# Layer 1's attention: GpSimd issues each half group's eight gathers only when the half group ahead has landed

## The chip, the core and the metric

The kernel runs on one core of a Trainium2 chip. A core has five engines that run their own instruction streams side by side and meet only at semaphores: TensorE (PE, matrix products and transposes, with weight loads shown as PEld), VectorE (DVE), ScalarE (ACT), GpSimd (POOL) and SyncE (SP, which here only issues DMAs). Sixteen DMA engines move data between HBM and the on-chip memory. The metric is the device time of one execution in microseconds (us). Before the change the median of three runs is 1322.91 us (1320.9 to 1323.34).

## The reference

Two layers work on 128 graphs of 64 nodes with 256 features, which is 8192 tokens. Each layer is a graph attention and a mixture of experts, both added to their input:

```python
# --- layer 0 ---
x = x + _L0_gnn_ref(_layernorm(x), adj, L0_gnn_W, L0_gnn_a)
x = x + _L0_ffn_ref(_layernorm(x), router_w, w1, b1, w2, b2)   # 8 experts, best 2, hidden 256, gelu
# --- layer 1 ---
x = x + _L1_gnn_ref(_layernorm(x), adj, L1_gnn_W, L1_gnn_a)
x = x + _L1_ffn_ref(_layernorm(x), Wg, bg, bias, W1, b1, W2, b2)  # 8 experts, best 2, hidden 512, relu

def _L1_gnn_ref(x, adj, W, a):
    Wh = jnp.einsum('bnf,fo->bno', x, W)
    a1, a2 = (a[:F_out, 0], a[F_out:, 0])
    e = (Wh @ a1)[:, :, None] + (Wh @ a2)[:, None, :]
    e = jnp.where(e > 0, e, ALPHA * e)
    attention = softmax(jnp.where(adj > 0, e, NEG_BIG), axis=-1)
    return elu(jnp.einsum('bij,bjo->bio', attention, Wh))
```

The change sits where layer 0 ends and layer 1's attention begins: x after layer 0 is x plus, for each token, its two best experts' outputs, each multiplied by its gate.

## The kernel before, in words

All tokens stay on the chip in the array X, in 64 tiles of 128 tokens (two graphs a tile). A group is 8 tiles, a half group is 4; there are 8 groups and 16 half groups.

Layer 0's experts write their outputs into a table in HBM, `expert_outputs` (`yslots` in the code), sorted by expert. Layer 1's attention begins with the way back. For each tile t and each of the two choices k, `gather_outputs` lets GpSimd issue one indirect DMA (L597) that fetches 128 rows of 256 floats, 128 KiB, into a ring of 16 tiles in the array WREG (`ring0`). That is 8 gathers for a half group and 128 in all. Four semaphores `y_gathered` are used in turn, one for a half group, and each gather adds 16 to its own, so that 8 gathers add 128. From the 17th tile on, every second tile waits at L594 for a transposition on TensorE (`xT_mm`), since a place in the ring is free only when its old tile has been added and transposed. GpSimd issues groups in order. Behind group 1 it writes two small tables (`one_hot_rows`, L605), and behind groups 3 to 7 it computes the low part of one expert weight (`low_part`, L611).

VectorE takes a half group with `add_outputs` (L1275 to L1287): it waits until the half group's semaphore shows all eight gathers, multiplies and adds the four tiles' first choices, then their second choices, and gives the mean to ScalarE. ScalarE sums the squares (`squares`, L1037), VectorE makes the inverse root (`first_rstd`, L1316 to L1325), and TensorE transposes (`turn_x`, L769) and projects (`project`, L782). ScalarE scales the projected rows (`scale_rows`, L1021).

VectorE's program has a fixed order. It takes half groups 0, 1, 2 and 3 (with the inverse roots of group 0 between them) before its first softmax, that of group 0 (`soft`, L1336). Within group g it then takes the two half groups of group g + 2: the first behind the division of the probabilities (`normalise_probs`, L1350), the second behind the first `add_relu` (L1360). The text below numbers half groups from 0 to 15, so half group 2 is the first half of group 1, and group 2 is half groups 4 and 5.

Of the kernel before, what the change touches and what calls it, by code (L numbers as in the profile page):

```python
# [61 lines left out]
def at(n):  # L62

    return n + AHEAD


def build(nc, x_in, adj, W_gnn, a_gnn, router, gate_b, gate_bias, w1, b1, w2, b2, out):

    ctx = ExitStack()
    with ctx:  # L70
# [3 lines left out]
        def sem(name):  # L74
            return ctx.enter_context(nc.semaphore(name))
# [143 lines left out]
        y_gathered = [sem(f"y_gathered_{k}") for k in range(4)]  # L219
# [288 lines left out]
        def _(pool):  # L508
# [56 lines left out]
            for L in range(2):  # L565
# [24 lines left out]
                def gather_outputs(g):  # L590

                    for t in range(g * GT, (g + 1) * GT):
                        if t >= 2 * GT and t % 2 == 0:
                            pool.wait_ge(xT_mm[1], at((t - 12) // 2 + 1))  # L594
                        for k in range(TOPK):
                            o = (TOPK * (t % (2 * GT)) + k) * D
                            nc.gpsimd.indirect_dma_start(  # L597
                                out=ring0[:, o:o + D], out_offset=None, in_=yslots,
                                in_offset=bass.IndirectOffsetOnAxis(ap=pos_i[k][:, t:t + 1].bitcast(U32), axis=0)
                            ).then_inc(y_gathered[t // 4 % 4], 16)  # L600
# [12 lines left out]
                if L == 0:  # L613
                    inverse_root(0)
                    no_edges(0)
                    inverse_root(1)
                    diagonal(0)
                    no_edges(1)
                    later_constants()
                    for g in range(1, GROUPS):  # L620
                        diagonal(g)
                        if g + 1 < GROUPS:
                            inverse_root(g + 1)
                        if g + 1 < GROUPS:
                            no_edges(g + 1)
                        cut_weights(g - 1, 0)
                        cut_weights(g - 1, 1)
                    cut_weights(GROUPS - 1, 0)
                    cut_weights(GROUPS - 1, 1)
                    pool.wait_ge(setup_dve, 2)  # L630
                    one_hot_rows()
                else:
                    for u in range(SU):
                        pool.wait_ge(stored[u], 16 + 16 * (SLOTS[0] // SU))
                    for g in range(GROUPS):
                        gather_outputs(g)
                        if g == 1:
                            one_hot_rows()
                        if g >= 3:
                            low_part((g - 3) // 2, (g - 3) % 2)  # L640
                    for g in range(GROUPS - 3, GROUPS):
                        low_part(g // 2, g % 2)
# [1129 lines left out]
```

## Time and profile before

| | |
|---|---|
| Median of three runs | 1322.91 us |
| Lowest and highest | 1320.9, 1323.34 us |
| Span of the profiled execution | 1413.2 us |
| Mean granted TensorE clock | 0.870 |
| Busy in the span: PE, DVE, ACT, POOL | 77%, 68%, 39%, 49% |
| Gathers of L597 | 128, 991 ns each on average |

The span runs from the first to the last instruction of the one execution that was recorded; for that execution the profile gives no other time. It is 90.3 us longer than the median of the runs without a profile. A timeline row of the profile gives the start from the span's begin, the busy time, the engine, the line, the operation with output and input, how many instructions the row merges, and in brackets the idle time ahead of it and what ended it. Busy time of a gather on GpSimd is the time in which GpSimd writes its descriptors, not the transfer.

### The profile page before, as it was taken

Reading aid. Unit: us, or ns where it says so; the run is one execution under the profiler, and the core shown is the slowest. Engines: PE = TensorE matmul, PEld = TensorE weight load, DVE = VectorE, ACT = ScalarE, POOL = GpSimd, SP = SyncE. Lnnn points to the kernel's source line nnn. Section 1 sums busy time; section 2 is a strip of 40 time slices with the busy share of each in tenths; the row PEclk is TensorE's granted clock in tenths of the full one; section 3 lists DMA queues with packets and bytes.
Section 4 is the critical chain, followed back from the end, with each engine's and each line's share of the span. In section 5 each row is a group of like instructions: output and inputs, shape, how many; then the busy total and the mean of one; then the engine's idle time right before and its main releaser. Section 6 shows DMA issues by size and latency. Waiting matters only on the chain.

```text
span 1413.2 us, 31628 instructions
## 1 busy us (share of the span) xinstructions
PE 1090.2 (77%) x9392; PEld 894.5 (63%) x9393; DVE 963.9 (68%) x1851; ACT 550.3 (39%) x1229; POOL 696.6 (49%) x752
## 2 busy tenths in 40 slices
PE   6999482479999962556776486489999997799995
PEld 4777372468888852345564372377879886587774
DVE  4889688847777742568897888656666654466664
ACT  3666486422222211556776575022222222122221
POOL 3577681155555527546670380142533125776652
PEclk9999755589999995888889659599999998899998
DMA  9211151045555543234452553555767433443430
GB/s 283 55 46 39 60 179 60 13 120 158 160 157 158 163 131 102 71 83 139 117 158 59 162 181 104 47 168 163 209 178 177 138 110 113 128 129 119 122 111 12
DMA packets 126095, 172.53 MB, mean 122 GB/s; under 512 B 35109, under 2 KB 94000, under 8 KB 125744
## 3 DMA queue, kind: packets, MB, share of 16 engines
q0 software_dynamic: 28288, 83.03, 21.4%
q1 hardware_dynamic: 89504, 88.22, 19.9%
q10 hardware_dynamic: 8208, 0.07, 0.9%
q8 instruction: 53, 0.87, 0.3%
q14 instruction: 42, 0.34, 0.1%
HBM read 100.87 MB, written 71.44 MB: 122 GB/s over the span
## 4 chain that ended last, share of the span: by engine, by line
PE 52%; issue 19%; DVE 10%; POOL 5%; ACT 5%; another core or an unknown queue 4%; DMA 2%; SPq 1%; DVEq 1%; POOLq 0%; ACTq 0%
PE bank L964 20%; PE bank L978 18%; PE bank L782 5%; PE bank L947 4%; POOL arena L649 2%; ACT b_bc L1037 1%; PE bank L810 1%; DVE X L1279 1%; DVE arena L1623 1%; DVE stats L1269 1%; PE bank L900 1%; PE bank L800 1%; DMA stage_w<-in_L_ffn_W 1%; DVE arena L1624 1%
## 5 line engine op out<-in xcount | busy, mean ns | idle before, releaser
L1187 ACT ACTIVATE arena<-bank,b1T 128x256 f32<-128x256 f32 (+1 forms) x464 | 176.0, 457 | 565.2 <-PE bank L964 360.7
L964 PE MATMUL bank<-arena,WREG 128*128 128x256 f16 (+1 forms) x2784 | 323.8, 268 | 20.5 <-issue 17.9
L978 PE MATMUL bank<-WREG,arena 128*128 x2544 | 309.4, 275 | 35.8 <-issue 32.0
L978 PEld LDWEIGHTS bank<-WREG,arena 128*128 128x128 f16 x2544 | 247.1, 99 | 80.5 <-issue 48.8
L964 PEld LDWEIGHTS bank<-arena,WREG 128*128 x2784 | 253.0, 99 | 61.0 <-issue 31.6
L1693 DVE CAST arena<-arena 128x1024 f16<-128x1024 f32 (+1 forms) x140 | 83.9, 599 | 193.2 <-ACT arena L1187 154.8
L668 POOL DMA_INDIRECT arena<-split_tokens,gather_row x136 | 130.6, 960 | 148.7 <-PE bank L947 59.5
L782 PE MATMUL bank<-wg_sb,arena 128*128 128x258 f32 x512 | 142.9, 426 | 45.4 <-ACT arena L1010 29.0
L597 POOL DMA_INDIRECT WREG<-expert_outputs,pos_both x128 | 126.9, 991 | 99.4 <-PE bank L769 38.8
L679 POOL DMA_INDIRECT X<-token_rows,gather_row x72 | 73.5, 1021 | 176.0 <-DMA first_rows<-X 83.4
L782 PEld LDWEIGHTS bank<-wg_sb,arena 128*128 128x128 f32 x512 | 103.7, 212 | 71.8 <-ACT arena L1010 33.9
L1695 DVE TENSOR_TENSOR arena<-arena 128x1024 f16<-128x1024 f32 (+1 forms) x140 | 135.3, 966 | 4.8
L1705 DVE SCALAR_TENSOR_TENSOR arena<-bank,b_bc 128x512 f32<-128x512 f32 (+1 forms) x152 | 97.0, 645 | 50.6 <-PE bank L978 29.6
L679 POOL DMA_INDIRECT X<-first_rows,gather_row x72 | 75.8, 1052 | 87.6 <-DMA first_rows<-X 48.1
L1687 DVE COPY arena<-bank 128x1024 f16<-128x1024 f16 x140 | 95.4, 682 | 27.6 <-PE bank L947 11.8
L696 POOL DMA_INDIRECT out<-X,scatter_row x72 | 81.7, 1135 | 53.8 <-DVE X L1718 34.9
L1021 ACT ACTIVATE arena<-bank,minus_one,cols 128x258 f32<-128x258 f32 x128 | 71.0, 565 | 73.8 <-remote 28.4
L649 POOL TENSOR_TENSOR arena<-arena 128x512 f16<-128x512 f32 x64 | 75.6, 1192 | 45.1 <-DVE arena L1456 45.1
L861 PE MATMUL bank<-ident,arena 128*128 128x128 f16 x512 | 62.6, 298 | 38.4 <-POOL arena L649 37.6
L810 PE MATMUL bank<-arena 128*128 128x256 f32 x256 | 70.3, 411 | 17.6 <-ACT arena L1051 13.2
L1360 DVE SCALAR_TENSOR_TENSOR X<-bank,X 128x512 f32<-128x512 f32 x64 | 43.8, 685 | 51.9 <-ACT arena L1059 48.2
L1279 DVE SCALAR_TENSOR_TENSOR X<-WREG,cols,X 128x256 f32<-128x256 f32 x128 | 66.1, 574 | 17.4 <-DMA WREG<-expert_outputs,pos_both 15.6
(204 smaller groups left out, 1528.7 us busy)
## 6 DMA issues: line engine op xcount, KB each, us to landing
first_rows<-X SPq DMA_DIRECT2D x72, 257.0 KB, 4.6
expert_outputs<-arena SPq DMA_DIRECT2D x68, 256.0 KB
X<-in_x SPq DMA_DIRECT2D x16, 512.0 KB, 6.0
split_tokens<-arena SPq DMA_DIRECT2D x16, 512.0 KB, 2.9
stage_w<-in_L_ffn_W SPq DMA_DIRECT2D x16, 512.0 KB
token_rows<-X SPq DMA_DIRECT2D x8, 1024.0 KB
token_rows<-arena SPq DMA_DIRECT2D x16, 512.0 KB, 3.7
stage_w<-in_L_ffn_w SPq DMA_DIRECT2D x16, 256.0 KB, 2.7
```

The source lines that it names most:

```text
L597: nc.gpsimd.indirect_dma_start(out=ring0[:, o:o + D], out_offset=None, in_=yslots, in_offset=bass.IndirectOffsetOnAxis(ap=pos_i[k][:, t:t ...
L649: nc.gpsimd.tensor_tensor(y16_4[:, 2 * q:2 * q + 2, D:2 * D], y32_4[:, 2 * (q % 4):2 * (q % 4) + 2, :], y16_4[:, 2 * q:2 * q + 2, 0:D], AL ...
L668: nc.gpsimd.indirect_dma_start(out=gat[:, u * 512:(u + 1) * 512], out_offset=None, in_=table, in_offset=bass.IndirectOffsetOnAxis(ap=gathe ...
L679: nc.gpsimd.indirect_dma_start(out=token_row(ST * j + a, 0, ROW), out_offset=None, in_=first_rows if f else token_rows, in_offset=bass.Ind ...
L782: last = mm(Wh_bank(t), xT[:, b:b + P], wg(L, c, 0, WA), start=c == 0, stop=c == KC - 1)
L810: last = mm(bank[6 + q % 2][:, a * D:(a + 1) * D], probsT[:, j * P:(j + 1) * P], Wh[g % 2][:, j * WA:j * WA + D], start=True, stop=True)
L964: last = mm(hb, w1_at(L, ea, wh, kc, fc), tT[:, tb:tb + width], start=n == 0, stop=n == 3 * KC - 1)
L978: last = mm(ob[a], hsrc[:, h0:h0 + P], w2_at(L, e[a % len(e)], wh, fc), start=fc == 0 and n == 0, stop=fc == FC - 1 and n == 2)
L1187: ins = A(hid[:, h0:h0 + width], bank[2 + 2 * (u % 2) + fc // 2][:, b0:b0 + width], ACT.Gelu if L == 0 else ACT.Relu, bias=cut(b1T, ea * F ...
L1687: V.tensor_copy(tT[:, (u % 2) * 4 * SLOT:(u % 2 + 1) * 4 * SLOT], bank[u % 2][:].bitcast(F16)).then_inc(T_ev[L], 1)
L1695: tt(hid_lo[:, hb:hb + FC * SLOT], hid[:, hb:hb + FC * SLOT], hid_hi[:, hb:hb + FC * SLOT], ALU.subtract).then_inc(h_split[L], 1)
L1705: ins = stt(o_sb[:, o0:o0 + width].rearrange("p (a d) -> p a d", d=D), bank[6 + u % 2][:, a * width:(a + 1) * width].rearrange("p (a d) -> ...
```

## The change

Two lines are added to `gather_outputs`; nothing else changes. At each half group's first tile but the very first (15 times), GpSimd waits until the semaphore of the half group ahead shows all eight of its gathers.

```diff
@@ -590,6 +590,8 @@
                 def gather_outputs(g):
 
                     for t in range(g * GT, (g + 1) * GT):
+                        if t >= 4 and t % 4 == 0:
+                            pool.wait_ge(y_gathered[(t // 4 - 1) % 4], 128 * ((t // 4 - 1) // 4 + 1))
                         if t >= 2 * GT and t % 2 == 0:
                             pool.wait_ge(xT_mm[1], at((t - 12) // 2 + 1))
                         for k in range(TOPK):
```

No instruction moves on any engine. What changes is what GpSimd's gathers wait for. Before the change, GpSimd's program has the following rows from the start of layer 1 to the gathers of the 20th tile (`stored` are the semaphores of the stores to `expert_outputs`, `xT_mm_1` that of the transpositions, `x31` merges 31 equal rows):

```order
L597 DMA WREG<-expert_outputs,pos_both 128x256 [waits stored_2,stored_3,stored_1,stored_0]
L597 DMA WREG<-expert_outputs,pos_both 128x256 x31
L605 IOTA arena 128x256
L605 IOTA arena 128x288
L597 DMA WREG<-expert_outputs,pos_both 128x256 [waits xT_mm_1]
L597 DMA WREG<-expert_outputs,pos_both 128x256 x3
L597 DMA WREG<-expert_outputs,pos_both 128x256 [waits xT_mm_1]
L597 DMA WREG<-expert_outputs,pos_both 128x256 x3
```

After the change, the same stretch reads as follows; lines below the two new ones carry a number higher by 2, so the gather is L599 (`y_gathered_0` to `y_gathered_3` are the half groups' semaphores):

```order
L599 DMA WREG<-expert_outputs,pos_both 128x256 [waits stored_2,stored_3,stored_1,stored_0]
L599 DMA WREG<-expert_outputs,pos_both 128x256 x7
L599 DMA WREG<-expert_outputs,pos_both 128x256 [waits y_gathered_0]
L599 DMA WREG<-expert_outputs,pos_both 128x256 x7
L599 DMA WREG<-expert_outputs,pos_both 128x256 [waits y_gathered_1]
L599 DMA WREG<-expert_outputs,pos_both 128x256 x7
L599 DMA WREG<-expert_outputs,pos_both 128x256 [waits y_gathered_2]
L599 DMA WREG<-expert_outputs,pos_both 128x256 x7
L607 IOTA arena 128x256
L607 IOTA arena 128x288
L599 DMA WREG<-expert_outputs,pos_both 128x256 [waits xT_mm_1,y_gathered_3]
L599 DMA WREG<-expert_outputs,pos_both 128x256 x3
```

The unbroken row of 32 gathers is cut into four pieces of 8, and the gathers behind the small tables have two things to wait for. Further on, around the low part of a weight (L611 before, L613 after), GpSimd's rows after the change are:

```order
L599 DMA WREG<-expert_outputs,pos_both 128x256 [waits xT_mm_1,y_gathered_2]
L599 DMA WREG<-expert_outputs,pos_both 128x256 x3
L599 DMA WREG<-expert_outputs,pos_both 128x256 [waits xT_mm_1]
L599 DMA WREG<-expert_outputs,pos_both 128x256 x3
L613 TENSOR_TENSOR WREG<-stage_w,WREG 128x1024 [waits high_ready_1]
L599 DMA WREG<-expert_outputs,pos_both 128x256 [waits xT_mm_1,y_gathered_3]
L599 DMA WREG<-expert_outputs,pos_both 128x256 x3
```

There, every half group's first gather had a wait already and has a second one now; the low part stands between the two halves' boundary as before.

## Rows read from the trace of the kernel before

**Rows 1.** The page: length, and shares of the chain that ended last.

```profile
span 1413.2 us, 31628 instructions
...
PE 52%; issue 19%; DVE 10%; POOL 5%; ACT 5%; another core or an unknown queue 4%; DMA 2%; SPq 1%; DVEq 1%; POOLq 0%; ACTq 0%
```

**Rows 2.** Timeline of GpSimd, start of layer 1: the first 64 gathers.

```profile
522.89 0.94 POOL L597 DMA_INDIRECT WREG<-expert_outputs,pos_both  x1 [23.17 <-DMA expert_outputs<-arena]
...
531.64 0.95 POOL L597 DMA_INDIRECT WREG<-expert_outputs,pos_both  x1 [0.31 <-issue]
532.89 0.95 POOL L597 DMA_INDIRECT WREG<-expert_outputs,pos_both  x1 [0.30 <-issue]
...
561.91 0.94 POOL L597 DMA_INDIRECT WREG<-expert_outputs,pos_both  x1 [0.30 <-issue]
562.86 3.18 POOL L605 IOTA arena<- 128x256 bf16 x2
568.04 0.96 POOL L597 DMA_INDIRECT WREG<-expert_outputs,pos_both  x1 [2.00 <-remote]
...
576.94 1.06 POOL L597 DMA_INDIRECT WREG<-expert_outputs,pos_both  x1 [0.30 <-issue]
584.90 1.15 POOL L597 DMA_INDIRECT WREG<-expert_outputs,pos_both  x1 [6.90 <-PE bank L769]
```

**Rows 3.** Timeline of VectorE in the same stretch.

```profile
534.53 2.23 DVE L1279 SCALAR_TENSOR_TENSOR X<-WREG,cols,X 128x256 f32<-128x256 f32 x5 [13.57 <-DMA WREG<-expert_outputs,pos_both]
...
575.90 2.19 DVE L1279 SCALAR_TENSOR_TENSOR X<-WREG,cols,X 128x256 f32<-128x256 f32 x5
...
579.36 0.17 DVE L1287 TENSOR_SCALAR cols<-cols 128x4 f32<-128x4 f32 x1
583.81 0.69 DVE L1336 SCALAR_TENSOR_TENSOR arena<-no_edge,bank 128x512 f32<-128x512 uint8 x1 [4.29 <-PE bank L790]
```

**Rows 4.** The chain that ended last, in time order; last row: steady part.

```profile
543.83 9.87 another core or an unknown queue
...
554.29 9.90 another core or an unknown queue
...
564.78 2.94 another core or an unknown queue
...
568.21 2.06 ACT b_bc L1037 x8
...
593.60 14.37 another core or an unknown queue
...
726.58 0.22 another core or an unknown queue
```

**Rows 5.** Timeline of TensorE: the projections of group 0's first four tiles.

```profile
540.93 5.40 PE L782 MATMUL bank<-wg_sb,arena 128*128 128x258 f32 x16 [1.73 <-issue]
```

**Rows 6.** Timeline of ScalarE: the scaling of the second and third of these tiles.

```profile
553.72 0.56 ACT L1021 ACTIVATE arena<-bank,minus_one,cols 128x258 f32<-128x258 f32 x1 [9.89 <-remote]
564.21 0.57 ACT L1021 ACTIVATE arena<-bank,minus_one,cols 128x258 f32<-128x258 f32 x1 [9.92 <-remote]
```

**Rows 7.** Timeline of GpSimd in the steady part, groups 6 and 7.

```profile
699.44 0.95 POOL L597 DMA_INDIRECT WREG<-expert_outputs,pos_both  x1 [0.30 <-issue]
702.45 0.94 POOL L597 DMA_INDIRECT WREG<-expert_outputs,pos_both  x1 [2.06 <-PE bank L769]
...
711.96 0.95 POOL L597 DMA_INDIRECT WREG<-expert_outputs,pos_both  x1 [0.30 <-issue]
712.92 2.13 POOL L611 TENSOR_TENSOR WREG<-stage_w,WREG 128x1024 f16<-128x1024 f32 x1
715.22 0.97 POOL L597 DMA_INDIRECT WREG<-expert_outputs,pos_both  x1 [0.16 <-issue]
```

**Rows 8.** Timeline of VectorE in the steady part, group 4's softmax to group 5's.

```profile
701.88 0.69 DVE L1336 SCALAR_TENSOR_TENSOR arena<-no_edge,bank 128x512 f32<-128x512 uint8 x1 [0.86 <-PE bank L790]
...
719.00 2.18 DVE L1279 SCALAR_TENSOR_TENSOR X<-WREG,cols,X 128x256 f32<-128x256 f32 x5
...
725.86 0.68 DVE L1336 SCALAR_TENSOR_TENSOR arena<-no_edge,bank 128x512 f32<-128x512 uint8 x1
```

**Rows 9.** Busy time by stretch (engine busy, count), TensorE clock, DMA share, GB/s.

```profile
702.00:727.00 25.00, 18.29 (x106) 14.02 (x104) 23.47 (x62) 18.93 (x47) 18.41 (x17) 0.93 0.52 148
```

## The prediction

> **What bounds the kernel now.** I read the page's head first, then the chain of waits over the start of layer 1, then the timelines of the engines there, and at last the same timelines in the steady part of the attention. The head gives the first warning: the profiled execution's span is 1413.2 us, while the median without a profile is 1322.91 us, so this one execution is 90.3 us longer than what is timed, and 4% of its chain (of 1413.2 us, so some 57 us) is put to "another core or an unknown queue", on a program that has one core [rows 1]. A sum on this trace has to say for each piece whether it is in the timed runs too.
>
> The start of layer 1 holds the most of those pieces: 9.87, 9.90, 2.94 and 14.37 us, together 37.1 us [rows 4]. One is plain to see: TensorE had its 16 projections done at 540.93 + 5.40 = 546.3 us [rows 5], and ScalarE, which waits for nothing else there, scaled the second of these tiles at 553.72 and the third at 564.21 [rows 6]. The signal took 9 to 18 us. Both stretches lie in bursts of gathers: GpSimd issued 32 of them without a pause from 522.89 to 561.91 [rows 2].
>
> The gathers themselves ran evenly. They start 1.25 us apart (531.64 and 532.89; 31 steps from 522.89 to 561.91 are 1.26 us each) [rows 2]. The eighth started at 531.64, and VectorE, which waits for just these eight, began at 534.53 [rows 2, 3]. So a half group has landed 2.9 us after its last gather starts. The first four half groups therefore land at about 534.5, 544.5, 554.5 and 564.8.
>
> **The change part by part.** It removes nothing and moves nothing; it adds 15 waits to GpSimd. Each turns the step between two half groups from 1.25 us (last gather to next gather) into 2.9 us or a little more. Behind each waiting instruction stand all later gathers and, from group 3 on, the low parts. I price one open boundary at 2.9 - 1.25 = 1.65 us and take 1.7, for GpSimd has to take up work again. The bounds from rows: 0.3 us at the least, if GpSimd sees the landing sooner than VectorE acts on it (the gather's own busy 0.95 us and as much again until the data is there would leave 1.9 - 1.25 = 0.65, and I allow half of that), and 2.9 us at the most, if nothing of the landing overlaps the next gather's issue.
>
> By the Trainium skill ("DMA: Bandwidth & Descriptors", the section "Anatomy of one DMA — SWDGE (gpsimd) path") a DMA issued by GpSimd takes about 2.0 us plus its bytes over 436 GB/s. For 131,072 bytes that is an estimate of 2.3 us, so a boundary would cost 1.05 us and the four that I count below 4.2 us instead of 6.8. The trace has 2.9 us for the same thing, and by it I go. The same page's rule to issue a DMA early and wait for it late speaks against this change, and it is the forecast's sign.
>
> Which boundaries are open:
>
> - *Half groups 0 to 3, three boundaries.* There is no other wait between them [rows 2]. Half group 3 lands 3 x 1.7 = 5.1 us later.
> - *Boundary 3 to 4.* The small tables take 3.18 us and another 2.00 us pass ahead of the next gather [rows 2]; 2.9 us of landing from the gather at 561.91 end at 564.8, before the tables do at 566.04. Hidden: 0.
> - *Boundary 4 to 5.* The trace has 6.90 us of waiting for a transposition there [rows 2], but that transposition is late because of the 37.1 us. Without them it is ready (half group 2 has been added by 558, and the transposition follows group 0's edge products, due by 564 as worked out below), and the boundary is open: 1.7.
> - *Boundary 5 to 6.* Open too, but half group 6 is wanted late: 0.
> - *Steady part.* The boundary in a group's middle: half group 12's last gather starts at 699.44 and has landed at 702.3; the next gather started at 702.45 anyway, 2.06 us idle for TensorE [rows 7]. The boundary between groups: last gather 711.96, landed 714.9; the low part of 2.13 us stands there, and the next gather started at 715.22 [rows 7]. Both hidden, just. Even a miss of some tenths costs nothing: half group 13, landed at 714.9, is taken at 719.00 [rows 7, 8], 4.1 us of slack.
>
> What waits for the open ones, in an execution without the 37.1 us:
>
> - VectorE must add half group 3 before its first softmax. The last half group's adds take 3.5 us (575.90 to 579.36) [rows 3], so this softmax can't start before 564.8 + 3.5 = 568.3. Its other input, group 0's edge products, comes from half group 1: landed 544.5, added by 548, and from the sum of squares behind that to the softmax it took 583.81 - 568.21 = 15.6 us [rows 3, 4], which gives 563.6. So half group 3 decides, by 4.7 us, and its delay goes on whole: 5.1 us.
> - In the middle of group 0 VectorE takes half group 5. In the steady part that point is 719.00 - 701.88 = 17.1 us behind the softmax's start [rows 8]; group 0 has no statistics and no remainder of a group ahead to work, some 5 us less by the length of those pieces, so 12 us, at 568.3 + 12 = 580. Half group 5 is the sixth: its gathers start no sooner than 568.04 + 8 x 1.25 = 578.0, the last at 586.8, and it has landed at 589.7. So gathers bound VectorE here too, and the delay that counts is that of half group 5: 5.1 + 1.7 = 6.8 us.
> - From group 1 on VectorE is busy 23.47 of 25 us [rows 9]; it can't catch up. GpSimd with its new waits needs 16 x 1.25 + 2 x 1.65 + what of the low part's 2.13 us the landing doesn't cover (0.5), 23.8 us, and keeps pace with 24.0 (725.86 - 701.88) [rows 8].
>
> Sum: 6.8 us, on the traced execution's own path only if its 37.1 us weren't there; on the median 1322.9 + 6.8 = 1329.7 us. Its own range from the bounds of a boundary: 4 x 0.3 = 1.2 to 4 x 2.9 = 11.6 us, so 1324 to 1334.5.
>
> **The rivals.**
>
> *Hidden: the late signals are in the timed runs as well, and the pauses don't mend them.* Then the softmax of group 0 waits for its edge products as in the trace: 583.81, while half group 3, added by 564.8 + 5.1 + 3.5 = 573.4, is in time, and half group 5 waits 6.90 us for TensorE as before. Time: 1323. For it: the trace is what there is. Against it: the 90.3 us that the profiled execution has too many must lie somewhere, and some 57 us of its chain are just such waits.
>
> *Faster: the late signals are in the timed runs, and the pauses mend them.* For it: in the steady part, with a pause of about 2 us in every 8 or 16 gathers, such waits are short (0.22 us on the chain at 726.58, for one), while the unbroken 32 and the later 16 have all 37.1 us [rows 2, 4]. It decides once pauses of 1.7 us are enough to drain what piles up. Gone would be up to 37.1 us less some 6 that stay, so 31, against 6.8 paid: 1322.9 - 31 + 6.8 = 1299 us. Half of it would be 1314. Against it: the same 90.3 us.
>
> On where the late signals come from, the Trainium skill ("NOTIFIC — the notification-queue block", 7.1 "Overflow: three behaviours, one of which stalls the engine") says that the block that carries trace records holds its producers back when its inner stages fill. That would make the waits the profile's own, and is no row of this trace.
>
> *Slower still: GpSimd becomes the bound.* If the other engines' period is shorter in the timed runs than the trace's 24.0 us, say by the share of late signals in it, GpSimd's 23.8 us rules. It decides below 23.8 us; at a period of 22.5 each of groups 1 to 5 costs 1.3 us more, 6.5 us in all: 1322.9 + 6.8 + 6.5 = 1336.
>
> *No wait in effect.* That the waits don't hold at all is out: each names the semaphore and the full count of the half group ahead.
>
> **How the numbers follow.** A measurement of this kernel can tell 0.2%, 2.6 us, from no change: 1320.3 to 1325.5. The forecast has 0.60, hidden 0.16, faster 0.15, slower still 0.09. Of the forecast's cases some 0.05 fall within 0.2% (cheap boundaries). So slower 0.64, same 0.21, faster 0.15. The predicted time is the forecast's, 1329.7. The range of 8 in 10 takes in the hidden case and half of the slower one: 1320 to 1335.
>
> **What would show each step.** In the changed kernel's profile the first gather of half groups 1, 2 and 3 should start about 2.9 to 3.0 us behind the gather ahead of it, not 1.25, with VectorE's or the landing's name or "DMA" as what ended the wait; the 32nd gather at about 567 instead of 561.9; the first gather behind the tables unmoved against them; in the steady part, the middle boundary's wait still ended by TensorE. The profiled span itself may well fall, since the pauses can shorten the late signals that the recorded execution has: if they vanish there, it is near 1413 - 31 + 7 = 1389 while the median rises. A median that falls with the span would prove the faster rival; an unchanged median with unshortened late signals, the hidden one. The forecast is wrong in its main step if the timed median moves less than 2.6 us although the 32nd gather is 5 us late, for then half group 3 or 5 doesn't decide.

## The result, and the profile after

The change makes the kernel slower by about one per cent. After it the median is 1336.22 us (1333.45 to 1338.79, four runs), and of the kernel before, beside it, 1321.91 us (1320.68 to 1323.34, four runs): a ratio of 1.0102, 95% interval 1.0085 to 1.0118, which is 13.5 us. The forecast was 1329.7 us, a change of 6.8; half of what happened was in it, and 1336.2 lies outside the range of 1320 to 1335. In some stretches of time, called disturbed below, every execution of the kernel before takes 1396 to 1421 us instead of 1322, and the profile shown ahead of the prediction is of that kind while the timed runs beside it are not.

The page of the changed kernel, its span and the shares of its chain:

```profile
span 1331.5 us, 31640 instructions
...
PE 47%; issue 18%; DVE 15%; POOL 10%; DMA 4%; ACT 4%; SPq 1%; POOLq 0%; DVEq 0%; ACTq 0%
```

The span is 1331.5 us and fits the timed runs. The 4% for another core or an unknown queue [rows 1] are gone. So this page can't be held against rows 1 to 9 line by line; where a number of before is needed, I take it from a second profile of the unedited kernel (the first experiment), with a span of 1318.6 us. The two spans differ by 12.9 us, as the medians do by 13.5.

GpSimd at the start of layer 1, after the change:

```profile
517.44 0.95 POOL L599 DMA_INDIRECT WREG<-expert_outputs,pos_both  x1 [0.30 <-issue]
520.53 1.16 POOL L599 DMA_INDIRECT WREG<-expert_outputs,pos_both  x1 [2.14 <-DMA WREG<-expert_outputs,pos_both]
...
544.44 1.15 POOL L599 DMA_INDIRECT WREG<-expert_outputs,pos_both  x1 [2.02 <-DMA WREG<-expert_outputs,pos_both]
...
553.41 0.95 POOL L599 DMA_INDIRECT WREG<-expert_outputs,pos_both  x1 [0.30 <-issue]
554.36 3.18 POOL L607 IOTA arena<- 128x256 bf16 x2
557.72 1.11 POOL L599 DMA_INDIRECT WREG<-expert_outputs,pos_both  x1 [0.17 <-issue]
...
569.65 1.15 POOL L599 DMA_INDIRECT WREG<-expert_outputs,pos_both  x1 [2.00 <-DMA WREG<-expert_outputs,pos_both]
```

The first gather of half groups 1, 2, 3 and 5 now waits 2.00 to 2.14 us for the landing, where that of half group 1 had 0.30 [rows 2]; that of half group 4 does not, for it stands behind the two small tables. A step over a boundary is 520.53 - 517.44 = 3.09 us. VectorE in the same stretch takes each half group when it lands:

```profile
520.39 2.19 DVE L1281 SCALAR_TENSOR_TENSOR X<-WREG,cols,X 128x256 f32<-128x256 f32 x5 [13.65 <-DMA WREG<-expert_outputs,pos_both]
...
556.32 2.19 DVE L1281 SCALAR_TENSOR_TENSOR X<-WREG,cols,X 128x256 f32<-128x256 f32 x5 [8.22 <-DMA WREG<-expert_outputs,pos_both]
559.86 0.69 DVE L1338 SCALAR_TENSOR_TENSOR arena<-no_edge,bank 128x512 f32<-128x512 uint8 x1
...
569.50 2.19 DVE L1281 SCALAR_TENSOR_TENSOR X<-WREG,cols,X 128x256 f32<-128x256 f32 x5 [2.67 <-DMA WREG<-expert_outputs,pos_both]
```

GpSimd in the steady part, the last gather ahead of each wait and the first behind it:

```profile
615.99 1.14 POOL L599 DMA_INDIRECT WREG<-expert_outputs,pos_both  x1 [0.30 <-issue]
619.19 0.94 POOL L599 DMA_INDIRECT WREG<-expert_outputs,pos_both  x1 [2.05 <-DMA WREG<-expert_outputs,pos_both]
...
628.02 0.95 POOL L599 DMA_INDIRECT WREG<-expert_outputs,pos_both  x1 [0.30 <-issue]
628.99 2.13 POOL L613 TENSOR_TENSOR WREG<-stage_w,WREG 128x1024 f16<-128x1024 f32 x1
631.70 0.96 POOL L599 DMA_INDIRECT WREG<-expert_outputs,pos_both  x1 [0.58 <-DMA WREG<-expert_outputs,pos_both]
...
644.32 0.94 POOL L599 DMA_INDIRECT WREG<-expert_outputs,pos_both  x1 [2.10 <-DMA WREG<-expert_outputs,pos_both]
```

The wait in a group's middle is ended by the landing (2.05 and 2.10 us), not by TensorE as in [rows 7], and behind the low part another 0.58 us go to it. From 619.19 to 644.32 are 25.13 us in which GpSimd does nothing but gathers, one low part and these two waits: it is the engine that sets the pace. From 606.75 to 693.72 no other engine keeps a gather waiting for longer than the 0.30 us that stand ahead of every gather. The stretches of one group each, from softmax to softmax (us, then busy time of PE, PEld, DVE, ACT and POOL, the granted clock, the DMA share and GB/s):

```profile
613.46:638.54 25.08, 17.80 (x100) 13.48 (x100) 23.14 (x62) 18.61 (x47) 18.16 (x18) 0.93 0.53 147
638.54:663.76 25.22, 17.54 (x100) 13.36 (x100) 23.23 (x62) 18.61 (x47) 17.99 (x18) 0.93 0.53 147
```

These answer to [rows 9]. VectorE is busy 23.1 to 23.2 of them, but not by its own work alone:

```profile
628.60 2.56 DVE L1289 TENSOR_SCALAR cols<-cols 128x4 f32<-128x4 f32 x1
...
631.68 0.48 DVE L1281 SCALAR_TENSOR_TENSOR X<-WREG,cols,X 128x256 f32<-128x256 f32 x1
```

The first row is an instruction on 128x4 numbers, which takes 0.36 us at 635.12, behind the other half group. Here it lasts 2.56 us, to 631.16, and the low part on GpSimd ends at 628.99 + 2.13 = 631.12. It counts as busy, and by its end it is a wait for GpSimd: beside the low parts at 603.85, 654.06 and 679.29 the same instruction takes 2.58, 2.56 and 2.57 us and ends within 0.04 us of each.

By the Trainium skill ("SBUF — State Buffer", "Who interferes with whom") VectorE and GpSimd share a pair of memory ports, the pair is locked for a whole instruction, and `tensor_scalar` is among the operations that can take it. The trace agrees in that the wait ends 0.04 us behind the low part; that VectorE's row begins 0.39 us ahead of the low part's is not explained by it.

### The profile page after: what moved, and what is told of

Same layout as the page of the kernel before. It is cut to its first block, busy times and chain, and to the rows that moved or that the text cites. A ratio compares the mean times of both kernels' runs of the same rounds, so it can differ in the third digit from the quotient of the medians.

```text
span 1331.5 us, 31640 instructions
## 1 busy us (share of the span) xinstructions
PE 1064.2 (80%) x9392; PEld 889.7 (67%) x9393; DVE 959.4 (72%) x1851; ACT 550.5 (41%) x1229; POOL 706.0 (53%) x752
## 3 DMA queue, kind: packets, MB, share of 16 engines
q0 software_dynamic: 28288, 83.03, 23.8%
## 4 chain that ended last, share of the span: by engine, by line
PE 47%; issue 18%; DVE 15%; POOL 10%; DMA 4%; ACT 4%; SPq 1%; POOLq 0%; DVEq 0%; ACTq 0%
PE bank L966 19%; PE bank L980 19%; PE bank L949 4%; POOL WREG L599 3%; DVE X L1281 3%; PE bank L784 2%; ACT b_bc L1039 2%; POOL arena L651 2%; DVE stats L1271 2%; POOL X L681 1%; DVE arena L1625 1%; DVE X L1369 1%; DVE X L1362 1%; DVE cols L1289 1%; DMA X<-first_rows,gather_row 1%
## 5 line engine op out<-in xcount | busy, mean ns | idle before, releaser
L966 PE MATMUL bank<-arena,WREG 128*128 128x256 f16 (+1 forms) x2784 | 312.0, 267 | 2.7 <-DVE arena L1689 2.7
L980 PE MATMUL bank<-WREG,arena 128*128 x2544 | 300.9, 273 | 16.3 <-issue 11.5
L980 PEld LDWEIGHTS bank<-WREG,arena 128*128 128x128 f16 x2544 | 245.5, 98 | 52.8 <-issue 23.1
L670 POOL DMA_INDIRECT arena<-split_tokens,gather_row x136 | 134.6, 990 | 132.5 <-DVE gather_row L1666 56.4
L599 POOL DMA_INDIRECT WREG<-expert_outputs,pos_both x128 | 126.0, 984 | 81.1 <-issue 33.2
L681 POOL DMA_INDIRECT X<-first_rows,gather_row x72 | 81.3, 1129 | 72.9 <-DMA first_rows<-X 48.5
L698 POOL DMA_INDIRECT out<-X,scatter_row x72 | 78.5, 1090 | 36.2 <-issue 19.2
L1281 DVE SCALAR_TENSOR_TENSOR X<-WREG,cols,X 128x256 f32<-128x256 f32 x128 | 53.9, 479 | 38.5 <-DMA WREG<-expert_outputs,pos_both 37.9
L812 PEld LDWEIGHTS bank<-arena 128*128 128x128 f32 x256 | 51.0, 206 | 39.2 <-issue 29.5
```

Of the source, the lines that this page charges most:

```text
L599: nc.gpsimd.indirect_dma_start(out=ring0[:, o:o + D], out_offset=None, in_=yslots, in_offset=bass.IndirectOffsetOnAxis(ap=pos_i[k][:, t:t ...
L670: nc.gpsimd.indirect_dma_start(out=gat[:, u * 512:(u + 1) * 512], out_offset=None, in_=table, in_offset=bass.IndirectOffsetOnAxis(ap=gathe ...
L681: nc.gpsimd.indirect_dma_start(out=token_row(ST * j + a, 0, ROW), out_offset=None, in_=first_rows if f else token_rows, in_offset=bass.Ind ...
L812: last = mm(bank[6 + q % 2][:, a * D:(a + 1) * D], probsT[:, j * P:(j + 1) * P], Wh[g % 2][:, j * WA:j * WA + D], start=True, stop=True)
L966: last = mm(hb, w1_at(L, ea, wh, kc, fc), tT[:, tb:tb + width], start=n == 0, stop=n == 3 * KC - 1)
L980: last = mm(ob[a], hsrc[:, h0:h0 + P], w2_at(L, e[a % len(e)], wh, fc), start=fc == 0 and n == 0, stop=fc == FC - 1 and n == 2)
```

## The experiments

Each kernel is the one before with the edit shown, but for the repeated change. Kernels of a group ran on one chip beside runs of the kernel before. 

**First group: the start and the steady part apart.** Before: 1322.21 us (21 runs).

`e1_before_again` has no edit.

> The kernel before once more, unedited, for an undisturbed profile. If the late signals were the recorded execution's own: ratio 1.000, a span of about 1318 to 1320 us, no 'another core or an unknown queue' in the chain over the start of layer 1, first softmax of layer 1 (L1336) 45.5 us after the first gather, half group 5 landed some 64 us after it. If they belong to every execution, the span is near 1413 us again. On the steady part: theory 'GpSimd paces the changed kernel' expects the softmaxes of groups 1 to 6 here 23.0 to 24.0 us apart (25.1 us in the changed kernel); theory 'all is lost at the start' expects 25.1 us here too.

Measured: 1322.26 us, ratio 1.0002 (0.9989 to 1.0016), span 1318.6 us. The page has no share for an unknown queue any more:

```profile
span 1318.6 us, 31628 instructions
...
PE 51%; issue 17%; POOL 12%; DVE 10%; DMA 5%; ACT 3%; SPq 1%; POOLq 0%; DVEq 0%; ACTq 0%
```

This is what the prediction should have been read from. GpSimd and two of its groups in the steady part:

```profile
616.59 0.94 POOL L597 DMA_INDIRECT WREG<-expert_outputs,pos_both  x1 [0.31 <-issue]
617.55 2.14 POOL L611 TENSOR_TENSOR WREG<-stage_w,WREG 128x1024 f16<-128x1024 f32 x1
619.85 0.97 POOL L597 DMA_INDIRECT WREG<-expert_outputs,pos_both  x1 [0.16 <-issue]
...
631.17 0.94 POOL L597 DMA_INDIRECT WREG<-expert_outputs,pos_both  x1 [1.24 <-PE bank L769]
...
655.17 0.94 POOL L597 DMA_INDIRECT WREG<-expert_outputs,pos_both  x1 [1.11 <-PE bank L769]
```

```profile
607.04:631.14 24.10, 18.30 (x100) 14.48 (x100) 21.56 (x62) 18.72 (x47) 18.45 (x17) 0.86 0.59 158
631.14:654.61 23.47, 17.85 (x97) 13.93 (x96) 21.52 (x62) 18.73 (x47) 18.44 (x17) 0.85 0.53 153
```

A group takes 24.10 and 23.47 us, and in it GpSimd waits for TensorE 1.24 and 1.11 us, of which 0.30 is there ahead of every gather; at 606.78 it is 0.30 and at 678.85, one group on, 1.51. So GpSimd had 0 to 1.2 us to spare in a group, not the 1.76 us that are left of the 2.06 in [rows 7].

`e2_start_three`, `e3_start_five` and `e4_late_only` have the wait at half groups 1 to 3, 1 to 5, and 6 to 15:

```diff
+                        if 4 <= t <= 12 and t % 4 == 0:       # e2_start_three
+                        if 4 <= t <= 20 and t % 4 == 0:       # e3_start_five
+                        if t >= 24 and t % 4 == 0:            # e4_late_only
+                            pool.wait_ge(y_gathered[(t // 4 - 1) % 4], 128 * ((t // 4 - 1) // 4 + 1))
```

> Only the waits ahead of half groups 1, 2 and 3. By the changed kernel's profile a boundary costs 2.05 us (last gather to the second of the next half group 4.55 us, not 2.50), so half group 3 and the first softmax are 6.1 us late. Theory 'start plus GpSimd's pace': +6 us, ratio 1.0045. Theory 'all at the start': +10 us or more, 1.008.

> The waits ahead of half groups 1 to 5. Boundary 3 to 4 lies under the small tables, boundary 4 to 5 is open. Theory 'start plus GpSimd's pace': four open boundaries of 2.05 us, +8 us, ratio 1.006, and a steady period as in the kernel before. Theory 'all at the start': +14 us, 1.0105, the whole change.

> Only the waits from half group 6 on; the start as before. Theory 'start plus GpSimd's pace': GpSimd needs 25.1 us for a group as in the changed kernel; it starts with the lead it has, so the loss is 5 groups x (25.1 less the old period of about 24) less that lead: +3 to +6 us, ratio 1.002 to 1.0045. Theory 'all at the start', and the prediction's own step on the steady part: 0, ratio 1.000.

Measured: 1327.33 us, 1.0035 (1.0021 to 1.0048); 1330.81 us, 1.0061 (1.0047 to 1.0074); 1330.2 us, 1.0060 (1.0039 to 1.0080). In microseconds 4.6, 8.1 and 7.9. The start costs what the prediction said (5.1 for three boundaries, 6.8 for five). The steady part alone costs as much again, where the prediction had nothing. The two add up to 16.0 us where the whole change costs 13.5; their intervals allow that.

**Second group: the two boundaries of the steady part, in a disturbed stretch.** Before: 1408.07 us (29 runs).

```diff
+                        if t >= 28 and t % 8 == 4:            # e5_middle_only
+                        if t >= 24 and t % 8 == 0:            # e6_between_only
+                            pool.wait_ge(y_gathered[(t // 4 - 1) % 4], 128 * ((t // 4 - 1) // 4 + 1))
```

`e7_own_work` waits for nothing, but gives GpSimd a small instruction more in the middle of groups 3 to 7; `e8_two_behind` waits for the half group before last:

```diff
+        spin = sb("spin", [P, 256], BF16)                     # e7_own_work
...
+                        if t >= 28 and t % 8 == 4:
+                            step(nc.gpsimd.iota(spin[:], pattern=[[1, 256]], base=0, channel_multiplier=0,
+                                                allow_small_or_imprecise_dtypes=True))
...
+                        if t >= 8 and t % 4 == 0:             # e8_two_behind
+                            pool.wait_ge(y_gathered[(t // 4 - 2) % 4], 128 * ((t // 4 - 2) // 4 + 1))
```

> Only the waits at a group's middle (ahead of half groups 7, 9, 11, 13, 15). Theory 'GpSimd paces the groups': in the changed kernel a group's 25.15 us on GpSimd are 16 gathers, 2.05 us of waiting at the middle, the low part and 0.77 us behind it; without the wait behind the low part it is 24.4 us at least, against 24.1 to 23.5 in the undisturbed kernel before: +2 to +5 us, ratio 1.003. Rival 'only the landing behind the low part is late': 0, ratio 1.000.

> Only the waits between groups from half group 6 on (ahead of half groups 6, 8, 10, 12, 14), each but the first behind a low part. Theory 'GpSimd paces the groups': GpSimd needs 25.15 - 2.05 = 23.1 us and waits for TensorE at the middle as before: 0 to +2 us, ratio 1.001. Rival 'only the landing behind the low part is late': all of the late waits' 8 us, ratio 1.006.

> The kernel before, no landing wait at all; GpSimd writes a small table of its own (256 numbers a partition, about 1.6 us and its signal) ahead of half groups 7, 9, 11, 13 and 15, where e5 has its waits. It adds work that the kernel doesn't need and leaves none out. Theory 'GpSimd paces the groups': as e5 less a little, +1.5 to +4 us, ratio 1.002 to 1.003. Rival 'it is the landing, what is in flight, not GpSimd's time': 0.

> The change with the wait one half group further back: GpSimd waits for the half group before the one ahead, so up to 16 gathers are under way. That one has landed 7 us before GpSimd asks. Theory 'the price is the landing that nothing overlaps': 0, ratio 1.000, first softmax 45.8 us after the first gather as in the undisturbed kernel before. Rival 'the waits cost by their number': +3 us or more.

Measured: 1414.71 us, 1.006 (1.0025 to 1.0095); 1407.44 us, 0.9994 (0.9965 to 1.0023); 1420.71 us, 1.0107 (1.0052 to 1.0163); 1422.14 us, 1.0092 (1.0064 to 1.0120). None of this says what happens at 1322 us, but it settles one thing. All 29 executions of the kernel before take 1396 to 1419 us here, and the profile of `e5_middle_only`, which has no wait ahead of half group 7, shows the stalls of [rows 1, 6] again:

```profile
PE 54%; issue 20%; DVE 8%; POOL 6%; ACT 5%; another core or an unknown queue 4%; DMA 2%; SPq 1%; DVEq 1%; POOLq 0%; ACTq 0%
```

```profile
552.25 0.57 ACT L1023 ACTIVATE arena<-bank,minus_one,cols 128x258 f32<-128x258 f32 x1 [9.19 <-remote]
562.74 0.57 ACT L1023 ACTIVATE arena<-bank,minus_one,cols 128x258 f32<-128x258 f32 x1 [9.92 <-remote]
```

The timed executions share what lengthens the profiled one, and the recording alone does not make the late signals, since the profile of e1 has none. Whether pauses mend them was not tested: e5, e6 and e8 leave the first 32 gathers in one unbroken row (0.30 us ahead of each), as the kernel before does. Why the wait two half groups back costs 0.9% here, though it costs nothing in the next group, was not followed up.

**Third group: the same boundaries again, and the change again.** Before: 1323.5 us (29 runs), on the chip of the second group. The edits of `e9_middle_again`, `e10_between_again` and `e11_two_behind_again` are those of `e5_middle_only`, `e6_between_only` and `e8_two_behind`; `e12_change_again` is the change.

> The waits at a group's middle alone (ahead of half groups 7, 9, 11, 13, 15), once more, since the call before ran on a chip on which the kernel before takes 1408 us and signals come late as in the first profile. On a chip of the 1322 us kind, theory 'GpSimd paces the groups': +2 to +5 us, ratio 1.003, softmaxes of groups 1 to 5 some 24.5 us apart. Rival 'only the landing behind the low part is late': 1.000.

> The waits between groups from half group 6 on alone, once more. On a chip of the 1322 us kind, theory 'GpSimd paces the groups': 0 to +2 us, ratio 1.001. Rival 'only the landing behind the low part is late': +8 us, 1.006. On a chip of the 1408 us kind again 1.000, with the softmax of group 1 some 12 us earlier and the later groups longer.

> The wait one half group further back, once more. On a chip of the 1322 us kind: ratio 1.000, every start as in the kernel before. On a chip of the 1408 us kind 1.009 again, which has then nothing to do with landings.

> The changed kernel beside the others on one chip. On a chip of the 1322 us kind 1.0102 again, +13 to +14 us: half from the start (e3), half from the steady part (e4), with the sum of both 16 us less what they share. On a chip of the 1408 us kind: its pauses shorten the late signals of the start, so faster than before, some 1380 to 1400 us, if pauses mend them; 1.010 if they do not.

Measured: 1326.37 us, 1.0025 (1.0012 to 1.0038); 1327.03 us, 1.0027 (1.0015 to 1.0039); 1323.48 us, 1.0000 (0.9984 to 1.0015); 1333.99 us, 1.0078 (1.0061 to 1.0096). The change measured again costs 10.3 us (8.1 to 12.7), which overlaps the first comparison's 11.2 to 15.6; added to 1322.9 us it would lie inside the stated range, so how far the number was off is less sure than which step failed. Either boundary of the steady part costs something by itself, 3.3 and 3.6 us. A wait that is already met when GpSimd comes to it costs nothing, so the price is the emptied pipeline and not the waiting instruction. Groups 1 to 4 take 24.84 to 24.94 us in e9 and 25.09 to 25.18 in e10, where e11, which costs nothing, has 23.49 to 24.55; so in the traces either boundary alone brings a group almost to the 25.1 of both. In the middle only, GpSimd has these rows, and VectorE the one below them:

```profile
610.81 0.94 POOL L599 DMA_INDIRECT WREG<-expert_outputs,pos_both  x1 [1.99 <-DMA WREG<-expert_outputs,pos_both]
...
621.28 2.15 POOL L613 TENSOR_TENSOR WREG<-stage_w,WREG 128x1024 f16<-128x1024 f32 x1
```

```profile
620.84 2.89 DVE L1281 SCALAR_TENSOR_TENSOR X<-WREG,cols,X 128x256 f32<-128x256 f32 x1
```

Between groups only:

```profile
620.98 0.95 POOL L599 DMA_INDIRECT WREG<-expert_outputs,pos_both  x1 [0.31 <-issue]
...
626.29 1.05 POOL L599 DMA_INDIRECT WREG<-expert_outputs,pos_both  x1 [2.21 <-DMA WREG<-expert_outputs,pos_both]
```

There the landing ends not 2.9 but over 5 us behind the last gather (626.29 - 620.98 = 5.31), and the wait behind the low part is 2.21 us where the prediction had 0.5. The fifth group shows why.

**Fourth group, again disturbed.** Before: 1411.19 us (33 runs). `e13_own_work_again` has the edit of `e7_own_work`; `e14_low_earlier` issues the low part ahead of the last tile's two gathers; `e15_tables_last` issues the small tables behind group 7 instead of group 1; `e16_all_three` joins the last two and adds a wait for x of group 5 ahead of the last three low parts.

```diff
+                        if t % GT == GT - 1 and g >= 3:       # e14_low_earlier
+                            low_part((g - 3) // 2, (g - 3) % 2)
...
-                        if g >= 3:
-                            low_part((g - 3) // 2, (g - 3) % 2)
...
-                        if g == 1:                            # e15_tables_last
+                        if g == GROUPS - 1:
...
+                        if g == GROUPS - 3:                   # e16_all_three
+                            pool.wait_ge(x_done[1], at(4 * (g + 1)))
```

> The kernel before with about 1.6 us of GpSimd's own work (a small table that nothing reads) ahead of half groups 7, 9, 11, 13 and 15 and no landing wait. The kernel before is to take 1322 us in this call; where it takes 1408, the call tells nothing. Theory 'GpSimd has under 1 us to spare in a group, and what is more pushes the low part into VectorE's adds': +2 to +4 us, ratio 1.0015 to 1.003, VectorE's stalled instruction 2.2 us or more, softmaxes 24.5 us apart. Rival 'the landing': 1.000.

> The kernel before with the low part of groups 3 to 7 issued ahead of the group's last tile, two gathers (2.5 us) sooner; nothing is waited for that wasn't. Theory 'the low part's place': it then lies under VectorE's statistics (eight instructions, 2.6 us) and no longer beside the adds, the stalled instruction falls from 1.25 to about 0.5 us: -3 to -5 us, ratio 0.997. Rival 'the low part costs VectorE the same wherever it is': 1.000.

> The kernel before with the small tables (3.2 us of GpSimd and 1.1 us around them) written behind the last group's gathers instead of behind group 1's. Theory 'the start is bound by the gathers up to half group 5': half group 5 lands 3.1 us sooner, so does the softmax of group 1: -3.1 us, ratio 0.9977. Rival 'the start is bound by half group 3 alone, the rest has slack': 1.000.

> Both moves together, and the second low part of the last group's pair held back until VectorE's next statistics. By the theories above the sum: -3.1 for the tables, -3 to -5 for the low parts, -2 for the pair that stalls one instruction 3.3 us: -8 us, ratio 0.994. If the moves undo each other, since GpSimd's time in a group is all used: -3 us.

Measured: 1421.19 us, 1.0083 (1.0052 to 1.0114); 1420.16 us, 1.0043 (1.0006 to 1.0080); 1410.98 us, 0.9986 (0.9956 to 1.0016); 1420.41 us, 1.0055 (1.0025 to 1.0086). These times say nothing of the kernel at 1322 us. They hold no version that is faster than the kernel before; e15's interval leaves 0.16% slower to 0.44% faster open.

**Fifth group: the low part and GpSimd's own work.** Before: 1322.95 us (23 runs). The edits are those of `e14_low_earlier` and `e7_own_work`.

> The kernel before, with no wait on a landing, but the low part of a weight is put directly behind the last gather of its group's first... of its group, ahead of the remaining statements of that step, which is the same place in GpSimd's order or an earlier one. Theory A (GpSimd's lateness reaches VectorE through the low part, which lengthens a small VectorE instruction beside it from 0.37 to 2.6 us, or from 1.25 to 2.9): the time goes with where the low part stands against VectorE's statistics; started under them it costs nothing, so -1 to +1 us against before; started under a small instruction it costs 1.3 us in each of five groups, +6. Theory B (the time is GpSimd's own sum of work in a group): the order doesn't matter, 0.

> The kernel before, with one more instruction on GpSimd (a 128x256 IOTA into a tile of its own, about 1.5 us) at the middle of groups 3 to 7 and no wait on a landing. Theory A (GpSimd has under 1 us to spare in a group of the steady part, so whatever it is given beyond that comes out at the end): +2 to +4 us, as the wait at the middle costs (+2.9). Theory B (the price of the wait at the middle lies in the gathers, which come in bursts with a gap, and not in GpSimd's time): 0 to +1 us.

Measured: `e17_low_at_once` 1328.02 us, 1.0042 (1.0022 to 1.0061), 5.5 us slower; `e18_own_work_last` 1325.47 us, 1.0021 (1.0001 to 1.0041), 2.8 us slower.

In e18 the extra instruction was smaller than expected, 0.36 us instead of 1.5:

```profile
632.28 0.36 POOL L595 IOTA spin<- 128x256 bf16 x1
```

Its interval reaches from 0.1 to 5.4 us. Nor does its trace show a loss in the steady part: the last softmax starts 217.3 us behind the first gather, against 215.7 in e1 and 217.7 in e11. So e18 decides nothing.

In e17 the time falls where the first theory put it (+6), but not by its mechanism alone. GpSimd, then VectorE, then the queue of SyncE, on which the finished group's 1 MB of x is stored (L455) and 512 KB of weights are loaded (L449):

```profile
616.86 2.14 POOL L613 TENSOR_TENSOR WREG<-stage_w,WREG 128x1024 f16<-128x1024 f32 x1
...
620.71 0.95 POOL L599 DMA_INDIRECT WREG<-expert_outputs,pos_both  x1 [0.31 <-issue]
...
636.33 0.94 POOL L599 DMA_INDIRECT WREG<-expert_outputs,pos_both  x1 [4.39 <-PE bank L769]
```

```profile
616.50 3.06 DVE L1354 TENSOR_TENSOR arena<-arena,soft_cols 128x512 f32<-128x512 f32 x1
...
629.44 2.19 DVE L1279 SCALAR_TENSOR_TENSOR X<-WREG,cols,X 128x256 f32<-128x256 f32 x5 [2.42 <-DMA WREG<-expert_outputs,pos_both]
```

```profile
620.19 0.39 SPq L455 DMA_DIRECT2D token_rows<-X  x1
620.62 0.58 SPq L449 DMA_DIRECT2D stage_w<-in_L_ffn_W  x1
```

The low part holds up the division (3.06 us instead of 0.69), so the store starts late, at 620.19, half a microsecond ahead of the half group's last gather at 620.71, and the load stands between the two. That gather has landed by 629.4, 8.7 us behind its start. VectorE waits 2.42 us for it, TensorE gets its tile later, and GpSimd then waits 4.39 us for TensorE. A group takes 27.3 us in this execution, which was 7.5 us longer than the median of its kernel. The store and the last gather meet in the unedited kernel too, at a smaller price; the load comes there only at 619.71, behind the gather:

```profile
616.09 0.39 SPq L455 DMA_DIRECT2D token_rows<-X  x1
```

```profile
624.31 2.19 DVE L1279 SCALAR_TENSOR_TENSOR X<-WREG,cols,X 128x256 f32<-128x256 f32 x5 [0.60 <-DMA WREG<-expert_outputs,pos_both]
```

Its last gather starts at 616.59, half a microsecond behind the store, and VectorE takes the half group 7.7 us later, having waited 0.60 us. Of the 128 arrivals that the trace records for that half group, 112 are in by 618.3; the last 16 come from 622.1 to 624.2, and the 16 arrivals of the store from 621.9 to 624.0. In e17 the last 16 come from 628.2 to 629.3, behind the store's (626.4 to 628.1) and beside the load's (628.0 to 629.5). After the change the store stands at:

```profile
622.53 0.39 SPq L455 DMA_DIRECT2D token_rows<-X  x1
```

That is 5.5 us ahead of the last gather (628.02), and its last arrival is 3.4 us behind its start: sooner than before, yet GpSimd now waits for it.

The runs moved the store against the last gather, and the landing moved with it. From the last gather's start to its half group's last arrival it takes:

| Store issued ahead of the last gather by | Landing of that gather |
|---|---|
| 0.5 us (e1, e11; 8 groups) | 6.8 to 8.0 us |
| 3.0 us (e10; 4 groups) | 4.7 to 5.8 us |
| 4.2 us (e9; 4 groups) | 3.6 to 5.0 us |
| 5.5 us (the change, e12, e4; 15 groups) | 2.8 to 4.0 us |
| no store within 9 us (e1) | 2.7 to 3.1 us |

On why a small gather should wait for a large store on another queue, the Trainium skill ("DMA: Bandwidth & Descriptors", "Queues, rings and completion order") says, where it treats the queues that SyncE uses, that a transfer's semaphore increment "lands only after every earlier write from that SDMA engine, across its queues". The arrivals above agree, since the late ones come in step with the last of the large transfers issued ahead of the gather. That the landing follows the store's place is shown by the table; that it does so by this mechanism is not.

## Why the prediction was half right

**What an open boundary costs: right.** 1.7 us was the term. The steps into half groups 1, 3 and 5 in the changed kernel are 3.09, 2.97 and 2.95 us against 1.25, so 1.7 to 1.8.

**Half group 3, three boundaries, 5.1 us: right.** From the first gather to the first softmax it takes 555.74 - 509.99 = 45.8 us in the clean kernel before and 559.86 - 508.69 = 51.2 after: 5.4. The 32nd gather is 553.41 - 508.69 = 44.7 us behind the first; "about 567" had been 44.1. The prediction's path to the first softmax (half group 3 lands, 3.5 us of adds) gave 45.4 for a kernel without late signals and without the change.

**Boundary 3 to 4 hidden, 4 to 5 open: right.** The first shows 0.17 us at 557.72, the second 2.00 us at 569.65. The second softmax is 7.1 us late (588.31 - 508.69 = 79.6, against 582.53 - 509.99 = 72.5), where 6.8 were forecast; e3, with only these waits, measured 8.1 (6.2 to 9.8).

**The steady part, "Both hidden, just": wrong, and this is the step that failed.** From the second softmax to the last one the changed kernel loses another 5.8 us; at the last it is 12.9 us late, counted from the first gather in both kernels. Its groups 1 to 4 take 25.15, 25.08, 25.22 and 25.07 us, those of the clean kernel before 24.50, 24.11, 23.46 and 23.65, and group 5 takes 26.91 against 25.38, by the starts of the softmaxes: 6.3 us in all, of which group 6 gives 0.5 back. A single trace is good to about 2 us here: against e11 the loss is 4.2 us, and the medians give 13.5 - 8.1 = 5.4. The step's sum was "23.8 us, and keeps pace with 24.0". The 24.0 was about right, and the 23.8 was 1.3 us too small:

- the seven steps inside a half group were 8.75 us and are 8.83 in one half (619.19 to 628.02) and 9.37 in the other (631.70 to 641.07), where single gathers take 1.0 to 1.2 us instead of 0.95; [rows 7] already had 711.96 - 702.45 = 9.51 for seven such steps;
- the middle step was 2.9 us and is 644.32 - 641.07 = 3.25;
- the step over the low part was 1.25 + 1.65 + 0.5 = 3.4 us and is 3.45 to 3.94 (3.68 in the rows above), since the store's transfer lies beside the landing.

8.83 + 3.68 + 9.37 + 3.25 = 25.13 us is the group that was measured, 1.1 us above 24.0. The cover failed with it: the step let TensorE's wait of 2.06 us [rows 7] swallow the middle boundary. That row came from the disturbed execution. In the clean one the wait is 0.30 to 1.51 us, and the steps inside a half group are about as long as after the change.

**The rival "slower still: GpSimd becomes the bound" describes the steady part.** It had 0.09, and 1336 us as its time. Its price of 6.5 us stands against 5.8 measured, which is partly luck: its condition was a group of 22.5 us against GpSimd's 23.8, and what happened was 23.5 to 24.5 against 25.1. The tests: e4, with waits in the steady part only, costs 7.9 us (5.2 to 10.6); e9 and e10 show that either boundary is enough to use up more than GpSimd's spare time; e11 that a met wait is free.

**How GpSimd's lateness reaches VectorE.** Outside the start, VectorE in the changed kernel shows no wait for a gather. It is held in the small instruction beside the low part, 2.56 us instead of 0.36, in each group. In the clean kernel before, the low part starts at 617.55, under the batch statistics, which it doesn't hold, and the first adds behind them lose only 0.8 us to it (2.96 us for five that take 2.19 elsewhere); in group 1 they lose 2.0 (4.22 us), and that group is also the one that the change lengthens least. But this is the way the delay travels and not its root: at 631.12, where the low part lets VectorE go, the half group that VectorE wants next has only just landed (VectorE 631.68, GpSimd 631.70). Without the hold VectorE would wait for the gathers in its place. That last sentence is argued from the rows; e17, meant to test it, changed what transfers stand beside the gathers as well and so left it open.

**The late signals.** The prediction held that they belong to the recorded execution, and gave the two rivals that deny it 0.31. The timed runs of before are free of them, and so the forecast rightly left out the 37.1 us. The reason was wrong: the timed executions of a disturbed stretch are as long as the profiled one, all of them. On one chip the kernel before took 1408 us (29 runs) and, seven minutes later, 1323.5 us (29 runs). The expected span "near 1389" was wrong with it; it is 1331.5. Of the 94.6 us between the two profiles of the unedited kernel, 12.9 lie ahead of the first gather, 36.1 between it and the last softmax and 45.6 behind. Its "9 to 18 us" for a signal is 7.4 to 17.9 by its own rows. The chance of mending stays open: no kernel with a pause in its first 32 gathers ran while signals were late. Where the signals are late from stays open too.

## What to carry to other kernels

A profile whose span doesn't fit the timed median gives durations of instructions, but not the idle time by which a step is called hidden. Price such a step as open, or take a second profile first: here the spare time was 0 to 1.2 us and not 1.8. An engine that waits for its own transfers to land pays the whole landing each time, 1.7 us more here than a plain step, and what stands behind it moves too: the low part came to lie beside other instructions, and the store beside other gathers. Waiting for the item before last instead cost nothing that could be measured at 1323.5 us (in the disturbed stretch it cost 0.9%), so where a limit on transfers in flight is wanted, put it one deeper.

## What the runs showed of the hardware that was not expected

- A gather of 128 KiB lands 2.7 to 3.1 us behind its start with no store near it, and 6.8 to 8.0 us when a 1 MB store was issued half a microsecond ahead of it (e1, e11); with a 512 KB load between the two, 8.3 to 8.9 (e17).
- While a low part of 2.13 us runs on GpSimd, VectorE instructions of 0.36, 0.48 and 0.69 us took 2.56, 2.89 and 3.06 us in the rows above; eight batch statistics beside one keep their 2.71 us.
- The first gather behind a wait for the landing is busy 1.14 to 1.16 us in 7 of the changed kernel's 14 cases, and 0.94 to 0.97 in the others.
